# The weighted sums of two attention slots made together, in a fused attention and expert kernel

## What is computed

```python
att = jnp.einsum('bhqd,bhkd->bhqk', q, k) * scale            # self: causal mask, softmax
y = jnp.einsum('bhqk,bhkd->bhqd', jax.nn.softmax(att, axis=-1), v)
attc = jnp.einsum('bhqd,bhkd->bhqk', qc, kc) * scale         # cross: 1601 keys
y = y + jnp.einsum('bhqk,bhkd->bhqd', jax.nn.softmax(attc, axis=-1), vc)
...
x = x + jnp.tanh(g_xattn[0]) * (y @ Wp + bp)
x = x + jnp.tanh(g_ffn[0]) * ffn(layernorm(x))               # top 4 of 32 experts, and a shared layer
```

## Time and profile before

| | us |
|---|---|
| median of 3 runs | 4881.16 |
| lowest, highest | 4878.72, 4891.64 |
| the profiled execution | 4891.12, span 4888.3 |

### The profile page before, as it was taken

How to read it: one execution, slowest core, us unless ns; L and a number is a source line. 1 busy time by engine, 2 the same in 40 slices (tenths; PEclk the granted TensorE clock), 3 DMA queues, 4 the chain that set the end, 5 groups by cost and what they waited for, 6 DMA issues and landing times. The chain is left out here.

```text
span 4888.3 us, 75159 instructions
## 1 busy us (share of the span) xinstructions
PE 4346.4 (89%) x25317; PEld 1904.0 (39%) x25317; DVE 3532.4 (72%) x7733; ACT 2694.8 (55%) x5523; POOL 1646.7 (34%) x2163
## 2 busy tenths in 40 slices
PE   5999999999999999999999999999999995588882
PEld 2333333333343434333333333333333332477771
DVE  5788788787878787878787877887877783244443
ACT  1665656565655556565656565656565653344441
POOL 1122323232323232323232222323232314388883
PEclk7999999999999999999999999999999997799996
DMA  5453545444444444544444444444444443888888
GB/s 115 71 91 73 111 79 104 81 109 78 106 79 100 79 102 77 109 82 109 82 105 85 98 87 97 83 98 90 97 94 97 93 96 118 178 151 150 149 150 244
DMA packets 363500, 513.22 MB, mean 105 GB/s; under 512 B 64124, under 2 KB 227820, under 8 KB 363176
## 3 DMA queue, kind: packets, MB, share of 16 engines
q1 hardware_dynamic: 272592, 385.16, 37.8%
q0 software_dynamic: 87728, 115.39, 13.3%
q10 hardware_dynamic: 2856, 8.52, 0.5%
HBM read 288.49 MB, written 201.27 MB: 100 GB/s over the span
## 5 line engine op out<-in xcount | busy, mean ns | idle before, releaser
L662 ACT ACTIVATE prob<-scores 128x512 f32<-128x512 f32 (+3 forms) x4352 | 2150.3, 561 | 1331.3 <-PE scores L467 1297.4
L849 DVE TENSOR_REDUCE pmx<-ring 128x1 f32<-128x512 f32 (+1 forms) x3328 | 1998.5, 661 | 188.9 <-PE ring L545 175.6
L467 PE MATMUL scores<-stacks 98*128 98x512 bf16 (+3 forms) x4352 | 1272.3, 369 | 70.5 <-ACT prob L662 41.1
L489 PE MATMUL outs<-prob,vt 128*32 128x512 f32 x8704 | 1096.7, 576 | 12.7 <-POOL prob L1051 11.7
L545 PE MATMUL ring<-stacks 96*128 96x512 bf16 x3072 | 984.4, 389 | 90.1 <-DVE pmx L849 80.7
L467 PEld LDWEIGHTS scores<-stacks 98*128 98x128 bf16 (+1 forms) x4352 | 338.5, 99 | 1244.3 <-ACT prob L662 718.7
L849 DVE TENSOR_REDUCE mc<-ring 128x1 f32<-128x128 f32 (+3 forms) x1024 | 437.1, 480 | 147.1 <-PE ring L562 112.1
L1573 POOL DMA_INDIRECT scratch_sums<-e_yo,e_tok x320 | 495.9, 1550 | 118.8 <-issue 86.2
L1051 POOL TENSOR_SCALAR_AFFINE_SELECT prob<-prob 128x512 f32<-128x512 f32 x256 | 167.9, 656 | 1077.0 <-ACT prob L662 1075.2
L545 PEld LDWEIGHTS ring<-stacks 96*128 96x128 bf16 x3072 | 303.2, 99 | 511.4 <-DVE pmx L849 243.8
L1121 POOL TENSOR_TENSOR split<-rest,split 128x512 bf16<-128x512 f32 (+1 forms) x224 | 218.5, 975 | 824.4 <-DVE split L943 823.9
(11 more groups left out here) (165 smaller groups left out, 3752.7 us busy)
## 6 DMA issues: line engine op xcount, KB each, us to landing
stacks<-scratch_parts SPq DMA_DIRECT2D x768, 128.0 KB, 7.1
stacks<-scratch_parts SPq DMA_DIRECT2D x384, 136.1 KB, 10.1
scratch_parts<-split SPq DMA_DIRECT2D x64, 768.0 KB, 4.5
e_xin<-scratch_slots SPq DMA_DIRECT2D x160, 289.0 KB
scratch_parts<-split SPq DMA_DIRECT2D x32, 816.8 KB, 4.4
num<-oc POOLq DMA_DIRECT2D x256, 64.0 KB
den<-scratch_inverses POOLq DMA_DIRECT2D x63, 256.0 KB, 8.9
ct<-in_ctx_t_dram SPq DMA_DIRECT2D x16, 800.5 KB, 8.2
```

The costliest lines, as they stand in the source:

```text
L467: eng.matmul(ps[0:m, k, q0:T], kst[g][0:KR + 2, j, k0:k0 + m], qst[g][0:KR + 2, j, qc + q0:qc + T], start=True, stop=True).then_inc(scored ...
L489: mm = eng.matmul(po[32 * j:32 * j + 32, q0:T], vt[ch][0:m, VW * vi + VE * hl:VW * vi + VE * hl + 32], prob[0:m, n % 2, j, q0:T], start=kt ...
L662: eng.activation(prob[0:m, n % 2, j, q0:T], ps[0:m, i % SB, q0:T], ACT.Exp, scale=SCALE).then_inc(exped.sem, 1)
L849: eng.tensor_reduce(dst, src, AX.X, ALU.max).then_inc(free_of(part, it), 1)
```

## The change

1. The weighted sums are no longer made at the end of each slot. `due` says which: in a quad (slots counted from its start) at the end of slots 2, 4, 6, 8, 10 and 12 those of the two slots before; at the end of slot 13 those of slot 12 alone; at the end of slot 15 those of 13 and 14; and at the end of the next quad's slot 0 those of 15 and 16. Slots 1, 3, 5, 7, 9, 11, 14 and 16 have none. Two sums of one call of `due` never lie across a change of `po`.
2. `prob` gets a third place, in `stacks`, and an exponential waits for the weighted sums of three slots before, not two.
3. The stacks have three places that the quads take in turn (`home`, `home_max`, `home_load`). The waits of the loads and of the row maxima's DMAs follow.
4. The experts' weights come in three portions, 11 experts and 8 in L, and 13 in X (before: 7, 8, 9 and 8).

```diff
-        return [[x] for x in f[:2] + [("spread",), ("experts", 3)] + f[2:10] + ROUTE + [("table",), ("fill", 0)] + f[10:]
+        return [[x] for x in f[:2] + [("spread",), ("experts", 2)] + f[2:10] + ROUTE + [("table",), ("fill", 0)] + f[10:]
...
-        deal(0, (36, 70, 104), [("experts", i) for i in range(3)], 0.0)
+        deal(0, (70, 104), [("experts", i) for i in range(2)], 0.0)
...
-PLACES = (((0, 2), (11, 16)), ((2, 5), (16, 21)), ((5, 8), (21, 27)), ((8, 11), (27, 32)))
+PLACES = (((9, 16), (28, 32)), ((16, 24),), ((0, 9), (24, 28)))
...
-        prob = sb("prob", [128, 2, 4, 512])
+        prob01 = sb("prob", [128, 2, 4, 512])
+        prob2 = stacks[:, 3 * (QW + KW):3 * (QW + KW) + 2 * 4 * 512].bitcast(F32).rearrange("p (h n) -> p h n", h=4)
...
+        home = lambda part, g: (4 * part.b + g) % 3
+        home_max = lambda part, g: (4 * (part.b + (g == 0 and part.kind != "P")) + g) % 3
+        home_load = lambda part, g: (4 * (part.b + (g < 2 and part.kind != "P")) + g) % 3
+
+        free_quads = (2, 3, 0, 1)
+
+        def prob(part, n):
+
+            i = (SLOTS * (part.b + (part.kind == "X")) + n) % 3
+            return prob2 if i == 2 else prob01[:, i, :, :]
+
+        def due(part, n):
+
+            r = n % (NCT + NQ)
+            first = n - 1 if r == NCT else n - 2 if r == NCT + 2 or r < NCT and r % 2 == 0 else n
+            return [i for i in range(first, n) if i >= 0 or not part.first]
...
-                    if n or not part.first:
-                        weighted(part, n - 1)
+                    for i in due(part, n):
+                        weighted(part, i)
...
-                    act.wait_ge(summed, part, n - 1)
-                    eng.activation(prob[0:m, n % 2, j, q0:T], ps[0:m, i % SB, q0:T], ACT.Exp, scale=SCALE).then_inc(exped.sem, 1)
+                    act.wait_ge(summed, part, n - 2)
+                    eng.activation(prob(part, n)[0:m, j, q0:T], ps[0:m, i % SB, q0:T], ACT.Exp, scale=SCALE).then_inc(exped.sem, 1)
...
                     if part.kind != "P":
-                        sp.wait_ge(scored, part, 4 * (NCT + NQ) * (g + 1) if ch == 0 else 0)
+                        sp.wait_ge(scored, part, 4 * (NCT + NQ) * free_quads[g])
...
-                    sp.wait_ge(scored, part, 4 * (NCT + NQ) * (i + 1) if part.kind == "L" else 0)
+                    sp.wait_ge(scored, part, 4 * (NCT + NQ) * (i + 2) if part.kind == "L" else 0)
+                    sp.wait_ge(summed, part, 0)
...
                     if part.kind != "P":
-                        sp.wait_ge(scored, part, 4 * (NCT + NQ) if g == 0 else 0)
+                        sp.wait_ge(scored, part, 4 * (NCT + NQ) * (2, 0, 0, 1)[g])
```

52 lines of the change are left out of this document (30 added, 22 removed).

## The result

| kernel | median of the runs | from to | span of the profiled execution | granted clock in it |
|---|---|---|---|---|
| before, on the same chip | 4882.83 us | 4878.72 to 4891.64 | 4888.3 us | 0.961 |
| changed | 5005.18 us | 5003.37 to 5009.96 | 5005.1 us | 0.957 |

The changed kernel takes 1.0249 of the time before, 95% interval 1.0237 to 1.0261: 122 us slower. The forecast was 4921, with a range up to 4960. Its sign was right, its size a third of what came.

The account below looks back on a forecast made before the run. TensorE was taken as the bound on average (busy 89%), VectorE in places. +2.5 us a batch times 15 is 37.5, with +3 for L a total of +41; from the median of 4881 the forecast was 4921 us, range 4842 to 4960.

Parts of the forecast that it names:

- What a merge saves on TensorE: Two sums in a row pay one entry and one exit: 0.19 us a merge, 32 merges per batch.
- the rival of 0.05: Between two sums TensorE pays exit and entry in full, so a merge saves nothing: 4966 us, chance 0.05.
- What a merge costs VectorE: Where VectorE is full, the four-bank ring runs dry behind a pair and VectorE stands for 0.84 us.
- Slots 14 to 27 and 31 to 34: Chains through VectorE start earlier or later: -0.9, +0.9, -1.3, +0.9 and, in 31 to 34, +1.35 us a batch.
- Slots 28, 29 and 50 to 63: Merges gain, with TensorE the bound in 50 to 63: -0.2 us in 28 and 29, -1.15 in 50 to 63.
- my upper end, 5014: 0.84 us lost instead of 0.19 won at six more merges a batch: +8.7 a batch, kernel 5014 us.
- Slots 35 to 49: Routing steps and maxima fill VectorE; five merges gain and lose nothing, those from 44 lose a little: +0.5 us.
- Slots 1 to 4, and 64 to 0: Slots 1 to 4 of a middle batch get shorter by 0.4 us; slots 64 to 67 and 0 stay the same.
- L: Batch L: three quads unchanged; in its last, two slots take 5.27 us instead of 4.80, six times: +3 us.
- The waits of TensorE: The time of TensorE's waits for VectorE ahead of ring matmuls would more than double.
- The factor 15: The change of a middle batch, +2.5 us, was multiplied by 15 batches (F and M): 37.5 us.
- X, the three places, the third buffer: Later expert loads in X, three places for the stacks and a third for exponentials: 0; X at most 25 us.

Follow-up runs that it names:

- short_pairs: The changed kernel, but each maximum reads only the first 256 of its 512 columns; 4673.96 us, ratio 0.9679 to the kernel before.
- routing_only: The changed kernel with pairs of sums only at the ends of slots 40, 42 and 44; 4924.38 us, ratio 1.0064 to the kernel before.
- fill: The changed kernel with each 512-column ring matmul of slots 40 to 44 made twice; 4924.53 us, ratio 1.0204 to the kernel before.
- single: The changed kernel without pairs, each sum made in the slot after its own as before; 4822.28 us, ratio 0.9976 to the kernel before.
- before_again: The kernel before, unchanged, run once more on a chip with halts; 4896.44 us (one run).
- single_again: The changed kernel without pairs, measured once more on a chip without halts; 4821.43 us, ratio 0.9982 to the kernel before.

## Why the forecast was wrong, by its own steps

**What a merge saves on TensorE**: right, a little small. The rows gave 0.19; the next scores start 1.86 after a pair and not 1.91, and where nothing else bounds (slots 20 and 21, 22 and 23, and 5 to 10 in short_pairs) a cycle is 0.24 shorter. That the merge does nothing, the rival of 0.05, is out: the second sum starts 0.88 us after the first.

**What a merge costs VectorE**: right. 0.84 a cycle was foreseen, 0.75 to 0.80 came in slots 5 to 10 (with 0.96 as VectorE's gap), the ring of three banks gave the 0.60 more that follows from the same sum, and the item ahead of the scores gave back 0.4. The fourth cycle (11 and 12) lost 0.08 where I had some 0.4.

**Slots 14 to 27 and 31 to 34**: right in sign and nearly in size, -1.26, +0.79, -1.66, +0.86 and +1.71, for -0.9, +0.9, -1.3, +0.9 and +1.35. That the gains at 17 and 25 are gains of order and not of the merge was tested: three pairs alone gain 1.3 in 16 and 17. No run takes apart the losses of 18 and 19, 26 and 27, and 31 to 34; for them the forecast's chains are borne out by size alone.

**Slots 28, 29 and 50 to 63**: this step failed. "Slots 28 and 29: -0.2" and "five merges at 0.19, two that save half: -1.15" measured +0.81 and +2.16. I priced these slots by VectorE's share of a stretch (38.32 of 50.85) and took TensorE for the bound. TensorE was the bound on the mean, but three cycles there hold a split item in which VectorE and the ring bank wait some 2 us for TensorE and ScalarE, and the single sum lay exactly over that. I had applied to the sum of slot 25 the question "what does it cover?", and did not ask it of the others. The price itself stood in my text: 0.84 lost instead of 0.19 won at six more merges was my upper end, 5014, called far because VectorE idles 15 to 25% there. Four cycles of it came in the traces of the result (0.81, 0.93, 0.83, 0.84), three on a chip without halts. That 5005 is so near to 5014 is partly chance, since 2 us a batch of it are the routing slots' below. The idle share was the wrong witness: in 28 and 29 of the changed kernel VectorE is busy 5.30 of 8.90, and TensorE waits for it all the same.

In slots 50 to 57 the two kinds of chip disagree: the pairs at 53 and at 51, 55 and 57 cost +0.93, -0.24, +0.02, -0.10 in the traces of the result, and -0.02, +0.17, +0.31, +0.47 on the chip without halts. Why they cost anything on the latter was not tried; short_pairs has -0.24 at 55 and 57, which points to VectorE's load.

**Slots 35 to 49**: this term failed as well, +2.52 for +0.5, and for a reason that the forecast doesn't have. It has the granted clock of 0.94 in the earlier trace rows and goes past it. With pairs TensorE stands more often between routing steps, the clock is at its lower level for some 9.5 us a batch and not 5, and the pair, two sums in one piece, falls into it (3.57 us and not 1.86). routing_only shows that the pairs there do it, fill that the clock makes most of the loss.

**Slots 1 to 4, and 64 to 0**: -0.2 for -0.4 and +0.1 for 0, as good as right. **L**: a slot pair in its last quad takes 5.21 us for a foreseen 5.27, 0.42 more than before; batch L 4.4 for 3 in the first traces, 10.7 on the later chip. **The waits of TensorE** for maxima ahead of 512-column ring matmuls were to more than double; they grew by half, from 80.7 to 123.2 us. **The factor 15** took the first batch for a middle one; it lost 3 there and 9 on the later chip. **X, the three places, the third buffer**: 0, as single showed. (4881 and 41 make 4922; the 1 us changes nothing.)

**The range** ended at 4960 since I left out what I called far. Most of what I had not looked at piece by piece (28, 29 and 35 to 63) then went the same way.

## What to carry to other kernels

Work of an engine that needs no ring bank is not only work: it is what the engine does while its consumer catches up. Before batching such work, list behind each piece what the next instruction would wait for if the piece were gone, place by place and not by busy shares of a stretch. Batch it only at the places where that wait is zero, or ends later anyway; here pairs at 11 places, 8 of the 32 and three moved by a slot, turned a loss of 2.4% into a gain of 1.65%. And where the granted clock is already below 1, look first at whether the new order makes TensorE stand more often there, and price the batched work at TensorE's lower level.

## What the runs showed of the hardware

**Halts on some chips only.** In two of the six sets of runs the kernel before takes 4883 and 4895 us, in the other four 4828 to 4832. The traces place the difference: slots 50 to 57 take 30.2 us in before_again and 25.9 in single_again, and outside them and the routing slots no slot differs by more than 0.2. The changed kernel itself takes 30.2 and 31.6 us there on the two chips with halts, and 26.8 on one without. Each chip was used in one set of runs, so that it is the chip and not the hour isn't shown. In slot 50 of the trace before, the exponential that follows two scores starts 1.75 us after them; below it the same in single, on another chip, where it starts 0.26 after them:

```profile
2293.43 0.28 PE L467 MATMUL scores<-stacks 98*128 98x128 bf16 x2
```
```profile
2295.18 0.28 ACT L662 ACTIVATE prob<-scores 128x128 f32<-128x128 f32 x1 [2.42 <-PE scores L467]
```
```profile
2269.35 0.28 PE L484 MATMUL scores<-stacks 98*128 98x128 bf16 x2
```
```profile
2269.61 0.45 ACT L683 ACTIVATE prob<-scores 128x128 f32<-128x128 f32 x2 [1.32 <-PE scores L484]
```

It happens while GpSimd issues the indirect stores of the routed rows, but they stand at the same place in single. What holds the engines up was not found.

**A VectorE operation beside GpSimd's.** The routing step L914 (128 x 128) takes 0.29 us in most places (52 of 64) and 2.21 when it meets GpSimd's product over 128 x 1024. The timeline of batch 5, VectorE's and GpSimd's:

```profile
1542.39 2.21 DVE L914 TENSOR_TENSOR split<-down,split 128x128 f32<-128x128 f32 x1
```
```profile
1542.11 2.35 POOL L1110 TENSOR_TENSOR num<-num,den 128x1024 f32<-128x1024 f32 x1 [8.88 <-DMA den<-scratch_inverses]
```

VectorE ends 0.14 us after GpSimd does, and what stands behind it on VectorE starts that much later. The Trainium skill, SBUF — State Buffer, says that a VectorE operation with two inputs in SBUF and a GpSimd operation that reads SBUF exclude each other for a whole instruction; L914 has two such inputs, and the trace agrees, with 2.21 for 0.29. Both kernels have it, in the slots in which the lower clock appears.
